# Two steps of TensorE swapped in each slot of a selective scan: the add of h*C before the turn of dt*x*B

## The chip, the cores and the metric

The kernel runs on one core of a Trainium2 chip. The metric is the device time of one execution in microseconds, median of the runs. A core has five engines with an instruction stream each: TensorE (PE in the rows, its weight loads PEld), VectorE (DVE), ScalarE (ACT), GpSimd (POOL) and SyncE (SP, which issues DMAs). They run side by side and meet only at semaphores that the kernel places by hand.

## The reference

A "macaron" layer on x of 4 batches x 512 tokens x 256 channels in float32: a mixture-of-experts FFN, a selective scan (Mamba), the same FFN again. The change is in the scan, of which this is the core:

```python
x_proj = x @ W_x.T
dt_x, Bm, Cm = jnp.split(x_proj, [R, R + N], axis=-1)      # R = 64, N = 16
dt = jax.nn.softplus(dt_x @ W_dt.T + b_dt)
A = -jnp.exp(A_log)
dA = jnp.exp(jnp.einsum('bld,dn->bldn', dt, A))
dBx = jnp.einsum('bld,bln,bld->bldn', dt, Bm, x)
def step(h, inp):
    dA_t, dBx_t, C_t = inp
    h = dA_t * h + dBx_t
    y_t = jnp.einsum('bdn,bn->bd', h, C_t)
    return (h, y_t)
...
y = ys.swapaxes(0, 1) + x * D
```

Around it: `x = x + 0.5 * ffn(layernorm(x))`, then `x = x + scan(layernorm(x))`, then `x = x + 0.5 * ffn(layernorm(x))`.

## The kernel before

The kernel has three stages: the first FFN (to some 183 us of the span), the scan (to some 399 us) and the second FFN. In the scan one batch is worked on after the other (b = 0 to 3), and in each batch one state after the other (n = 0 to 15). State s = 16b + n is one slot; there are 64. For each state, channels lie on the partitions in two halves (k) and 512 tokens lie along them, 1024 elements a partition.

The work of one state s goes over four engines:

- ScalarE (`ahead`, lines 499 to 503), three states on: `decay` makes da = exp(dt*A) (line 482), `outer` makes the product dt*x*B with tokens on the partitions, `dbx_t` (line 496). VectorE makes some of its four token tiles instead (line 998; the table `BY_DVE` says how many).
- TensorE `turn_dbx(s)` (line 730) transposes these four tiles, 8 transposes of 128x128, into one of two PSUM pairs, `DBX[s % 2]`. The pair is read by VectorE's scan of state s-2, so the turn waits for that scan (`sc_h`), and for the products.
- VectorE scans, h = da*h + dbx, over 128x1024 elements in one instruction (line 1012), into a ring of four buffers. It waits for the turn of its state (`sc_dbx`), for da, and for GpSimd to have read the ring buffer of state s-4 (`sc_g`).
- GpSimd multiplies h by C into one of two buffers `gs` (line 381). It waits for the scan, for C's row (a DMA), and for the add of state s-2 (`sc_tp`).
- TensorE `add(s)` (line 745) transposes this product back, again 8 transposes, and sums it over the states in the PSUM pair `YA`. It waits for GpSimd (`sc_g`), and in the first state of a batch for VectorE to have read the sum of the batch before (`sc_x`).

Only states 62 and 63 have their product from VectorE (line 1035). Each engine works through its stream in the written order. In TensorE's slot s (function `scan`, lines 758 to 779) stand: in some slots `project_bt` (n = 4, the B of the next batch turned, lines 691 to 698) or `route` (batch 3, n = 5 and 10, lines 572 to 581); then `turn_dbx(s + 2)`; then `add(s - 1)`; then in some slots more: `project_z` (n = 0, 1), `skip` (n = 3, x*D, 16 matmuls, line 755), `turn_dt` (n = 8, 10), the transposes of LayerNorm (n = 12, 13), `project` (n = 15).

VectorE's slot s: `outer(s + 2)` (its share), scan s, then in some slots more: `add_y` of the batch before (n = 1, line 1042, waits for the last add of that batch), its statistics (n = 2), `project_bt` (n = 4, the copy of the turned B, line 958), `project_w` and `project_dt` (n = 5 to 8, lines 967 to 977), `project_dtx` (n = 10, 12, line 983). GpSimd's slot has the product alone, except in batches 1 to 3 after n = 3: there it also makes the LayerNorm of the batch before (lines 339, 340 and four of line 346).

Of the kernel before, what the change touches and what calls it, by code (L numbers as in the profile page):

```python
# [27 lines left out]
def macaron_kernel(nc, x, w_xT, w_dtT, b_dt, a_log, d_skip, router_w, gate_w, up_w, down_w,  # L28
# [32 lines left out]
    with ExitStack() as ctx:  # L61
# [142 lines left out]
        def states_by(engine, s):  # L204

            return sum(engine in (("dve",) if v else ()) + (("act",) if v < LT else ()) for v in sum(BY_DVE, ())[0:s])

        def last_two(s):

            return s >= STATES - 2  # L210
# [340 lines left out]
        def _(pe):  # L551
            def ln_transposes(c, q):
                pe.wait_ge(ln_xn, GT * c + 2 * q + 2)
                if c == 2:
                    pe.wait_ge(ln_xnT, (GT // 2) * c + q)
                    pe.wait_ge(pj_dtx, 2 * min(q // 2 + 3, BATCH))
                elif c == 1 and q == 7:
                    pe.wait_ge(ln_xnT, GT // 2 + 7)
                elif q >= 2:
                    pe.wait_ge(ln_xnT, (GT // 2) * c + q - 1)  # L560
                dst = turn_bank(c, q)
                for i in range(2):
                    for k in range(KC):
                        last = nc.tensor.transpose(dst[:, (i * KC + k) * P:(i * KC + k + 1) * P],  # L564
                                                   xn[:, 2 * q + i, k * P:(k + 1) * P], ident[:])
                last.then_inc(ln_tp, 1)
# [5 lines left out]
            def route(r, b):  # L572
                c = 2 * r
                if r == 1:
                    pe.wait_ge(sc_dve, states_by("dve", min(N * (BATCH - 1) + (ROUTES + (N, N))[b] + 3, STATES)))
                pe.wait_ge(ln_xnT, (GT // 2) * c + 2 * b + 2)
                for i in range(LT * b, LT * (b + 1)):
                    for k in range(KC):
                        last = nc.tensor.matmul(LG[r][:, i, :], xnT[:, k, i * P:(i + 1) * P], w_rt[:, k, :],  # L579
                                                start=(k == 0), stop=(k == KC - 1))  # L580
                last.then_inc(rt_logits, 1)
# [99 lines left out]
            def project(b):  # L681
                lo = b * L
                pe.wait_ge(ln_xnT, GT // 2 + 2 * b + 2)
                if b > 0:
                    pe.wait_ge(ln_xnT, GT + 2 * max(b - 2, 0))
                    pe.wait_ge(pj_dtx, 2 * b)
                for k in range(KC):
                    mm = nc.tensor.matmul(pj_bank(b, 0)[0:R + 2 * N, :], w_x[:, k, :], xnT[:, k, lo:lo + L], start=(k == 0), stop=(k == KC - 1))  # L688
                mm.then_inc(pj_all, 1)

            def project_bt(b):

                pe.wait_ge(pj_copy, b + 1)
                if b > 0:
                    pe.wait_ge(sc_dve, states_by("dve", N * (b - 1) + 4 + 3))
                for i in range(LT):
                    mm = nc.tensor.transpose(B_T[:, b, i, :], proj[R:R + N, i * P:(i + 1) * P], ident[R:R + N, R:R + N])
                mm.then_inc(pj_bt, 1)

            def project_z(b, k):  # L700
                pe.wait_ge(pj_copy, b + 1)
                if b > 0 and k > 0:
                    pe.wait_ge(pj_max, KC * b + k)
                nc.tensor.matmul(pj_bank(b, k), w_dt[:, k * P:(k + 1) * P], proj[0:R], start=True, stop=True).then_inc(pj_z, 1)

            def turn_dt(b, h):

                pe.wait_ge(pj_dt, KC * (b + 1))
                if b > 0 and h > 0:
                    pe.wait_ge(pj_dtx, 2 * b + h)  # L710
                dst = YS[h] if b == 0 else T
                for i in range(2):
                    for k in range(KC):
                        lo = (b % 2) * L + (2 * h + i) * P
                        mm = nc.tensor.transpose(dst[:, (i * KC + k) * P:(i * KC + k + 1) * P], dt_sb[:, k, lo:lo + P], ident[:])
                mm.then_inc(pj_tp, 1)

            def turn_dbx(s):

                if s >= 2:  # L720
                    pe.wait_ge(sc_h, s - 1)
                elif s == 0:
                    pe.wait_ge(ln_xnT, GT // 2 + 6)
                else:
                    pe.wait_ge(pj_dtx, 2)
                pe.wait_ge(sc_act, states_by("act", s + 1))
                pe.wait_ge(sc_dve, states_by("dve", s + 1))
                for k in range(KC):
                    for i in range(LT):
                        mm = nc.tensor.transpose(DBX[s % 2][:, k, i * P:(i + 1) * P], dbx_t[:, s % TURNS, i, k * P:(k + 1) * P], ident[:])  # L730
                mm.then_inc(sc_dbx, 1)

            def add(s):

                products = gs
                if last_two(s):
                    products = last
                    pe.wait_ge(sc_last, s - (STATES - 3))
                else:
                    pe.wait_ge(sc_g, s + 1)  # L740
                if s % N == 0:
                    pe.wait_ge(sc_x, KC * (s // N))
                for k in range(KC):
                    for i in range(LT):
                        mm = nc.tensor.matmul(YA[k][:, i * P:(i + 1) * P], products[:, s % 2, k, i * P:(i + 1) * P], ident[:],  # L745
                                              start=(s % N == 0 and i == 0), stop=(s % N == N - 1), is_transpose=True, skip_group_check=True)
                mm.then_inc(sc_tp, 1)

            def skip(b):
                lo = b * L  # L750
                if b == 0:
                    pe.wait_ge(consts, 1 + KC)
                for k in range(KC):
                    for i in range(LT):
                        nc.tensor.matmul(YA[k][:, i * P:(i + 1) * P], xnT[:, k, lo + i * P:lo + (i + 1) * P], d_diag[:, k, :],
                                         start=False, stop=False, skip_group_check=True)

            def scan(b):
                more = b + 1 < BATCH
                for n in range(N):  # L760
                    s = N * b + n
                    if more and n == 4:
                        project_bt(b + 1)
                    if not more and n in ROUTES:
                        route(1, ROUTES.index(n))
                    if s + 2 < STATES:
                        turn_dbx(s + 2)
                    if s > 0:
                        add(s - 1)
                    if more and n in (0, 1):  # L770
                        project_z(b + 1, n)
                    if n == 3:
                        skip(b)
                    if more and n in (8, 10):
                        turn_dt(b + 1, (n - 8) // 2)
                    if b > 0 and n in (12, 13):
                        ln_transposes(2, 2 * (b - 1) + n - 12)
                    if n == N - 1 and b + 2 < BATCH:
                        project(b + 2)
# [28 lines left out]
            for b in range(BATCH):  # L808
                scan(b)
# [312 lines left out]
```

## Time and profile before

| what | value |
|---|---|
| runs of the kernel before | 549.12 us median of 3 (547.7 to 549.31) |
| the profiled execution | 548.21 us |
| its span, first to last instruction | 546.4 us |
| mean granted clock of TensorE | 0.926 |
| busy: TensorE, weight loads, VectorE, ScalarE, GpSimd | 80%, 55%, 64%, 47%, 47% |

The rows below come from this one profiled execution. A start is in us from the start of the span. The clock is the share of TensorE's full 2.4 GHz that was granted in a stretch; 0.50 is 1.2 GHz.

### The profile page before, as it was taken

The page shows a single profiled execution, that of the slowest core. Times are in us where ns is not written, and L with a number is a line of the kernel's source. Part 1 is how long each engine was busy: PE and PEld are TensorE (multiplying, and loading weights), DVE is VectorE, ACT ScalarE, POOL GpSimd, SP SyncE. Part 2 cuts the span into 40 slices and gives each one's busy share as a digit, 9 for nine tenths or more (in the row PEclk, how much of TensorE's full clock was granted, in tenths as well). Part 3 has the DMA queues.
Part 4 walks back from the last instruction along what each step waited for, and adds up shares of the span by engine and source line. Part 5 has one row for each costly group of instructions (what it writes and reads, how often), then busy time and mean ns, then how long its engine had stood idle before and what let it go on. Part 6 is the DMA issues. An engine that isn't in the chain of part 4 may idle for free.

```text
span 546.4 us, 7393 instructions
## 1 busy us (share of the span) xinstructions
PE 434.9 (80%) x2204; PEld 301.7 (55%) x2205; DVE 348.1 (64%) x592; ACT 257.6 (47%) x499; POOL 254.6 (47%) x198
## 2 busy tenths in 40 slices
PE   1989989999807477878768867777888998999960
PEld 1745655555404346765667667677763664555530
DVE  5385433343347968999799899997949433333424
ACT  1211122332205769999989999976411112223210
POOL 4117203223321136786979698879802700332230
PEclk9979999999966679899999989997998999999995
DMA  8997312226851012133233223412300331222119
GB/s 266 178 326 247 85 39 78 86 77 197 132 173 60 0 57 75 69 104 90 52 86 96 84 62 98 106 60 78 78 0 30 107 68 41 85 77 86 58 48 307
DMA packets 54188, 55.27 MB, mean 101 GB/s; under 512 B 16465, under 2 KB 43409, under 8 KB 54161
## 3 DMA queue, kind: packets, MB, share of 16 engines
q1 hardware_dynamic: 50416, 44.68, 30.2%
q0 software_dynamic: 3744, 10.24, 5.3%
q8 instruction: 15, 0.25, 0.2%
q14 instruction: 13, 0.10, 0.1%
HBM read 36.39 MB, written 18.52 MB: 100 GB/s over the span
## 4 chain that ended last, share of the span: by engine, by line
PE 53%; DVE 25%; issue 10%; DMA 4%; POOL 3%; ACT 3%; SPq 0%; DVEq 0%; POOLq 0%; ACTq 0%
PE bank L630 16%; DVE hs L1012 12%; PE bank L609 9%; PE bank L655 6%; PE bank L599 5%; PE bank L745 3%; PE bank L730 2%; PE bank L579 2%; DMA xn_no<-token_out 2%; PE bank L564 2%; DVE stats L832 2%; PE bank L688 2%; PE bank L641 2%; PE bank L646 2%; DVE dbx_t L998 2%
## 5 line engine op out<-in xcount | busy, mean ns | idle before, releaser
L381 POOL TENSOR_TENSOR gs<-hs,c_sb 128x1024 f32<-128x1024 f32 x62 | 146.2, 2372 | 43.6 <-DVE hs L1012 32.2
L1012 DVE TENSOR_TENSOR_SCAN hs<-da,bank 128x1024 f32<-128x1024 f32 x64 | 144.8, 2276 | 10.5 <-PE bank L730 10.5
L368 POOL DMA_INDIRECT token_out<-y_sb,row_token x46 | 44.0, 957 | 141.3 <-DVE y_sb L933 141.3
L730 PE MATMUL bank<-ident,dbx_t 128*128 128x128 f32 x512 | 74.0, 291 | 34.1 <-DVE hs L1012 29.3
L630 PE MATMUL bank<-w_gu,tt 128*128 x184 | 90.8, 616 | 3.9 <-ACT tt L433 3.0
L482 ACT ACTIVATE da<-dt_sb,a_neg 128x511 f32<-128x511 f32 x128 | 84.9, 712 | 9.0 <-DVE hs L1012 8.9
L730 PEld LDWEIGHTS bank<-ident,dbx_t 128*128 128x128 f32 x512 | 60.4, 149 | 50.4 <-DVE hs L1012 39.2
L496 ACT ACTIVATE dbx_t<-dtx_t,h_sb 128x256 f32<-128x256 f32 x194 | 83.7, 495 | 3.0 <-PE bank L730 3.0
L921 DVE SCALAR_TENSOR_TENSOR q_sb<-th,bank 128x256 f32<-128x256 f32 x46 | 19.4, 421 | 88.9 <-ACT th L428 88.9
L745 PE MATMUL bank<-ident,gs 128*128 128x128 f32 x496 | 68.7, 285 | 8.7 <-POOL gs L381 8.5
L428 ACT ACTIVATE th<-bank 128x256 f32<-128x256 f32 x46 | 17.6, 383 | 108.4 <-PE bank L630 108.4
L745 PEld LDWEIGHTS bank<-ident,gs 128*128 128x128 f32 x496 | 59.4, 148 | 10.8 <-POOL gs L381 10.4
L609 PE MATMUL bank<-xnT,w_gu 128*128 128x512 f32 x128 | 62.4, 642 | 0.4 <-DVE gs L852 0.4
L630 PEld LDWEIGHTS bank<-w_gu,tt 128*128 128x128 f32 x184 | 31.3, 189 | 40.2 <-issue 40.1
L357 POOL DMA_INDIRECT sorted_rows<-xn_no,slot x32 | 31.2, 975 | 46.5 <-DVE xn_no L895 37.7
L655 PE MATMUL bank<-w_dn,tt 128*128 x184 | 47.8, 382 | 2.5 <-DVE y_sb L933 1.4
L609 PEld LDWEIGHTS bank<-xnT,w_gu 128*128 128x128 f32 x128 | 26.1, 208 | 31.4 <-issue 29.4
L410 ACT ACTIVATE xnT<-bank 128x512 f32<-128x512 f32 x24 | 13.9, 592 | 59.2 <-PE bank L564 59.2
L564 PE MATMUL bank<-ident,xn_no 128*128 128x128 f32 x96 | 18.1, 338 | 29.8 <-DVE xn_no L842 29.0
L421 ACT ACTIVATE hs<-bank 128x512 f32<-128x512 f32 x16 | 9.5, 595 | 61.5 <-PE bank L609 61.5
L655 PEld LDWEIGHTS bank<-w_dn,tt 128*128 128x128 f32 x184 | 31.4, 190 | 6.3 <-issue 4.0
L433 ACT ACTIVATE tt<-bank 128x512 f32<-128x512 f32 (+1 forms) x50 | 28.1, 562 | 9.8 <-PE bank L646 6.2
(103 smaller groups left out, 484.2 us busy)
## 6 DMA issues: line engine op xcount, KB each, us to landing
c_sb<-c_dram SPq DMA_DIRECT2D x64, 256.0 KB, 3.3
sorted_rows<-zero_row SPq DMA_DIRECT2D x2, 2944.0 KB, 17.1
xg<-sorted_rows SPq DMA_DIRECT2D x46, 128.0 KB, 2.0
xn_no<-token_out SPq DMA_DIRECT2D x8, 512.0 KB, 5.6
x_sb<-in_x SPq DMA_DIRECT2D x4, 512.0 KB, 6.5
w_gu<-in_gate_w SPq DMA_DIRECT2D x2, 1024.0 KB, 14.8
w_gu<-in_up_w SPq DMA_DIRECT2D x2, 1024.0 KB, 11.9
w_dn<-in_down_w SPq DMA_DIRECT2D x2, 1024.0 KB, 13.4
```

The lines of the kernel that those rows point to most:

```text
L357: nc.gpsimd.indirect_dma_start(out=sorted_rows[r], out_offset=bass.IndirectOffsetOnAxis(ap=slot[:, i:i + 1], axis=0), in_=xn_no[:, i, :], ...
L368: nc.gpsimd.indirect_dma_start(out=token_out, out_offset=bass.IndirectOffsetOnAxis(ap=row_token[:, j:j + 1], axis=0), in_=y_sb[:, j % 4, : ...
L381: nc.gpsimd.tensor_tensor(gs[:, s % 2], hs[:, s % RING], c_sb[:, s % RING].unsqueeze(1).to_broadcast([P, KC, L]), ALU.mult).then_inc(sc_g, 1)
L482: nc.scalar.activation(da[:, s % RING, k, 1:L], dt_sb[:, k, seq(s // N)][:, 1:L], ACT.Exp, scale=a_neg[:, k, s % N:s % N + 1]).then_inc(sc ...
L496: step = nc.scalar.activation(dbx_t[:, s % TURNS, i, :], dtx_t[:, b % 2, i, :], ACT.Copy, scale=b_t[:, b, i, n:n + 1])
L564: last = nc.tensor.transpose(dst[:, (i * KC + k) * P:(i * KC + k + 1) * P], xn[:, 2 * q + i, k * P:(k + 1) * P], ident[:])
L609: last = nc.tensor.matmul(dst, w_gu[:, k, SHARED, w + fo * P:w + (fo + 1) * P], xnT[:, k, b * L:(b + 1) * L], start=(k == 0), stop=(k == K ...
L630: last = nc.tensor.matmul(H[j0 % 2][:, :], tt[:, j0 % 2, 2 + k], w_gu[:, k, bass.ds(e, 1), :].squeeze(1), start=(k == 0), stop=(k == KC - 1))
L655: last = nc.tensor.matmul(Y[:, 0:D], tt[:, j0 % 2, k], w_dn[:, k, bass.ds(e, 1), :].squeeze(1), start=(k == 0), stop=(k == KC - 1))
L730: mm = nc.tensor.transpose(DBX[s % 2][:, k, i * P:(i + 1) * P], dbx_t[:, s % TURNS, i, k * P:(k + 1) * P], ident[:])
L745: mm = nc.tensor.matmul(YA[k][:, i * P:(i + 1) * P], products[:, s % 2, k, i * P:(i + 1) * P], ident[:], start=(s % N == 0 and i == 0), st ...
L1012: nc.vector.tensor_tensor_scan(hs[:, s % RING].rearrange(flat), da[:, s % RING].rearrange(flat), DBX[s % 2][:, :, :].rearrange(flat), 0.0, ...
```

## The change

In each slot s of TensorE's `scan`, `add(s - 1)` now stands before `turn_dbx(s + 2)`. Both keep their own waits and instructions, and all other engines keep their streams.

```diff
@@ -763,10 +763,10 @@
                         project_bt(b + 1)
                     if not more and n in ROUTES:
                         route(1, ROUTES.index(n))
+                    if s > 0:
+                        add(s - 1)
                     if s + 2 < STATES:
                         turn_dbx(s + 2)
-                    if s > 0:
-                        add(s - 1)
                     if more and n in (0, 1):
                         project_z(b + 1, n)
                     if n == 3:
```

## Rows read from the trace of the kernel before

**Rows 1.** The page, part 1: busy us, share of the span, instructions.

```profile
PE 434.9 (80%) x2204; PEld 301.7 (55%) x2205; DVE 348.1 (64%) x592; ACT 257.6 (47%) x499; POOL 254.6 (47%) x198
```

**Rows 2.** Stretches, batches 1 to 3: start:end, length, each engine's busy time, clock, DMA.

```profile
250.00:302.00 52.00, 40.13 (x301) 34.01 (x300) 48.76 (x49) 47.82 (x93) 43.51 (x22) 0.97 0.34 82
302.00:353.00 51.00, 38.86 (x298) 33.96 (x299) 49.41 (x49) 48.99 (x96) 43.95 (x23) 0.97 0.32 89
353.00:399.00 46.00, 36.86 (x297) 34.41 (x295) 39.70 (x38) 29.24 (x59) 36.28 (x19) 0.93 0.25 69
```

**Rows 3.** Waits of VectorE, 183 to 399: who, for whom, us, times, longest.

```profile
DVE hs L1012 <- PE bank L730: 10.5, 5, 4.6
DVE h_sb L958 <- PE bank L697: 6.7, 3, 2.8
```

**Rows 4.** Timeline, boundary of batches 0 and 1: start, us, instruction, count, idle before.

```profile
249.60 1.28 DVE L1042 TENSOR_TENSOR x_sb<-x_sb,bank 128x512 f32<-128x512 f32 x2 [0.24 <-PE bank L745]
```

**Rows 5.** Timeline, batch 1, states 19 to 23.

```profile
255.61 2.28 DVE L1012 TENSOR_TENSOR_SCAN hs<-da,bank 128x1024 f32<-128x1024 f32 x1
...
257.95 1.97 PE L730 MATMUL bank<-ident,dbx_t 128*128 128x128 f32 x8 [2.48 <-DVE hs L1012]
257.97 2.37 POOL L381 TENSOR_TENSOR gs<-hs,c_sb 128x1024 f32<-128x1024 f32 x1 [2.10 <-DVE hs L1012]
...
261.16 1.95 PE L755 MATMUL bank<-q_sb,xnT 128*128 128x128 f32 x16
...
263.04 0.42 PE L697 MATMUL bank<-ident,th 16*128 16x16 f32 x4
...
263.50 0.23 DVE L958 COPY h_sb<-bank 128x64 f32<-128x64 f32 x1 [2.83 <-PE bank L697]
...
266.63 7.00 POOL L381 TENSOR_TENSOR gs<-hs,c_sb 128x1024 f32<-128x1024 f32 x3
...
267.74 2.28 DVE L1012 TENSOR_TENSOR_SCAN hs<-da,bank 128x1024 f32<-128x1024 f32 x1
269.04 1.09 PE L745 MATMUL bank<-ident,gs 128*128 128x128 f32 x8 [1.38 <-POOL gs L381]
...
271.25 2.27 DVE L1012 TENSOR_TENSOR_SCAN hs<-da,bank 128x1024 f32<-128x1024 f32 x1
```

**Rows 6.** Timeline, batch 2, states 35 to 39.

```profile
310.33 1.09 PE L730 MATMUL bank<-ident,dbx_t 128*128 128x128 f32 x8 [2.48 <-DVE hs L1012]
...
311.26 1.04 PE L745 MATMUL bank<-ident,gs 128*128 128x128 f32 x8
...
321.43 1.17 PE L745 MATMUL bank<-ident,gs 128*128 128x128 f32 x8 [2.80 <-POOL gs L381]
...
322.22 2.28 DVE L1012 TENSOR_TENSOR_SCAN hs<-da,bank 128x1024 f32<-128x1024 f32 x1
```

**Rows 7.** Timeline, batch 3, states 55 to 57.

```profile
367.73 1.07 PE L730 MATMUL bank<-ident,dbx_t 128*128 128x128 f32 x8
...
368.83 2.29 DVE L1012 TENSOR_TENSOR_SCAN hs<-da,bank 128x1024 f32<-128x1024 f32 x1 [0.44 <-PE bank L730]
...
371.78 1.97 PE L745 MATMUL bank<-ident,gs 128*128 128x128 f32 x8 [2.98 <-POOL gs L381]
373.54 1.91 PE L730 MATMUL bank<-ident,dbx_t 128*128 128x128 f32 x8
...
375.49 2.29 DVE L1012 TENSOR_TENSOR_SCAN hs<-da,bank 128x1024 f32<-128x1024 f32 x1 [4.06 <-PE bank L730]
...
378.02 2.29 DVE L1012 TENSOR_TENSOR_SCAN hs<-da,bank 128x1024 f32<-128x1024 f32 x1
```

**Rows 8.** Timeline, the end of the scan: state 60, then 61 to 63 merged.

```profile
385.80 2.29 DVE L1012 TENSOR_TENSOR_SCAN hs<-da,bank 128x1024 f32<-128x1024 f32 x1 [0.44 <-PE bank L730]
...
388.31 6.63 DVE L1012 TENSOR_TENSOR_SCAN hs<-da,bank 128x1024 f32<-128x1024 f32 x3
```

**Rows 9.** Stretch after the gap in batch 2: length, TensorE busy, granted clock, DMA.

```profile
322.40:325.70 3.30, 3.30 (x18) 0.50 0.44 113
```

## The prediction

> **What bounds the kernel now.** I first read the busy shares of the page: no engine is busy all the time, VectorE 64% of the span [rows 1]. The change touches only the selective scan, so the next view is the table of stretches, one for each batch of the scan. In the middle two batches VectorE is busy 49 of 51 to 52 us, GpSimd 44 and TensorE 40; in the last batch VectorE has only 39.7 of 46.0 [rows 2]. So the scan is paced by VectorE's own list, and what costs time is what makes VectorE wait. The table of waits lists these for the whole scan: 10.5 us for TensorE's turned products of line 730 (five times) and 6.7 us for the turned B of line 697 (three times) [rows 3]. All other waits on TensorE are free. The question is thus where `turn_dbx(s + 2)` comes later or earlier, and whether a VectorE scan is ready for it then.
>
> **The loop in rows.** I number states 0 to 63 (s = 16b + n). From the start of scan s to the start of what it releases (turn, product h*C) pass 2.34 us: 255.61 to 257.95 [rows 5]. From the start of a product to the start of its add pass 2.41 us: 266.63 to 269.04 [rows 5]. A block of 8 transposes at full clock moves the next block back by 0.93 us: 310.33 to 311.26 [rows 6]. From the start of a turn to the scan that waited for it pass 1.10 us: 367.73 to 368.83 [rows 7]. At half clock the two last terms together are read directly: add at 371.78, turn at 373.54, scan at 375.49, that is 3.71 us [rows 7], against 0.93 + 1.10 = 2.03 us at full clock.
>
> **What the change does in an undisturbed slot.** Before, turn s+2 waits for scan s alone. After, it also stands behind add s-1, and so behind product s-1. From the start of scan s-1: 2.34 + 2.41 + 2.03 = 6.78 us until scan s+2 can start. VectorE itself needs three scans with their outer products for this, at 2.53 us (375.49 to 378.02 [rows 7]) 7.59 us, more where it also has projection work. The tightest place is the last three scans: 388.31 + 6.63 - 2.28 = 392.66 us for the start of scan 63, less 385.80 for scan 60, 6.86 us [rows 8]. So the new wait is covered everywhere, in the end by under 0.1 us. In return adds move into TensorE's idle time before the scan's end. Cost of the undisturbed slots: 0. If this cover goes (TensorE at half clock, or a product 0.3 us late), the price is up to 1.7 us a slot.
>
> **Gain at batch boundaries.** In slots 16 and 32 the last add of a batch releases VectorE's addition of y (line 1042), which waits 0.24 us for it [rows 4]. Now this add comes before its turn (0.93 us earlier): -0.24 us, twice, since the row at 301.98 repeats it.
>
> **Gain at the turned B.** In slot 16b+3 add 16b+2 stands between turn 16b+5 and the skip matmuls, behind which come the turned B and VectorE's copy (line 958). The product for this add is done 2.10 us before scan 16b+3 ends (GpSimd's idle time before 257.97 [rows 5]), so the add moves into idle time. In batch 1 the copy at 263.50 comes at 257.95 - 0.24 + 0.93 + 1.88 + 0.46 = 260.98, where 1.88 is skip to turned B (261.16 to 263.04) and 0.46 turned B to copy (to 263.50) [rows 5]; half clock at 257.95 gave 1.97 us in place of 1.09 and is part of the 2.5 us. In batch 2 it gains 0.93 us. In batch 0 TensorE is behind anyway, both orders hold the same work ahead of the B, and the gain is 0.
>
> **Loss at GpSimd's LayerNorm.** In batches 1 to 3, after product 16b+3, GpSimd normalises the batch before (lines 340, 346): in batch 1 from the end of product 19 at 257.97 + 2.37 = 260.34 to 266.63, so product 16b+4 is 6.3 us late and its add starts at 269.04 [rows 5], 321.43 [rows 6] and 371.78 [rows 7]. Before, that add is behind turn 16b+7, and only turn 16b+8 is held up. After, turn 16b+7 is held up too, one scan earlier. VectorE is one scan less ahead of GpSimd, and this is where that counts.
>
> The clock decides the price. TensorE would now wait from turn 16b+6 until the add, about 6 us in batches 1 and 2 (batch 1: the B turned from 260.52, then add 19 and turn 22 until 262.8, then nothing until 268.8), and 4.9 in batch 3, where turn 55 no longer fills the gap. In the trace the gap of 2.80 us before 321.43 and that of 2.98 us before 371.78 were both followed by half the granted clock (0.50, the 1.2 GHz level; blocks of 1.9 us) for 3.3 us and more [rows 6, 7, 9]; in batch 1 the wait of 1.38 us was not [rows 5]. Longer gaps than those that did it, so I take 3.71 us in all three; the other end is 2.03. The Trainium skill ("TensorE: Matmul & The Clock Gate", section "Why this matters for your kernels") says that idle gaps between bursts throw TensorE back to half rate; the trace agrees at the two gaps named. By that rule the sum is the one below, without it the second rival's.
>
> Batch 1: scan 23 starts at 269.04 - 0.24 + 3.71 = 272.51, before 271.25: **+1.26** (boundary gain within; the gain at the turned B is gone, as scan 23 waits for TensorE in any case). After it VectorE has 3.51 us a slot (267.74 to 271.25) and nothing is late.
> Batch 2: the add starts 1.26 - 0.24 = 1.02 later, at 322.45, scan 39 at 326.16, before 322.22: 3.94, of which **+2.68** is new.
> Batch 3: it has no boundary gain, as TensorE has no projection there. The add starts at 371.78, now followed by turn 55 and not 56. So scan 55 starts at 375.49 in place of 368.83, and scan 56 follows by VectorE's pace at 378.02 in place of 375.49: **+2.53**. The old stall of 4.06 us is not repeated for scan 56, its turn is done by then. The rest of batch 3 keeps VectorE's pace: 0.
>
> Sum: 1.26 + 2.68 + 2.53 = +6.47 us. The profiled execution took 548.21 us with its span of 546.44 us, 0.9 below the median of 549.12. 548.21 + 6.47 = 554.7 in its terms, 555.6 in those of the median, 1.2% slower. The second FFN is not touched; its half-clock stretches may fall otherwise, which I put at 1 us either way (each of 3.3 us costs at most half of that).
>
> **Rivals.**
> 1. *The tight cover breaks* (slower still). The slack of under 0.1 us at the tail and of 0.8 elsewhere is gone wherever TensorE is at half clock: 6.78 + 1.68 = 8.46 against 7.59 us. For: the restarts leave it at half clock for a slot or two. Against: in batches 1 and 2 these slots hold 3.5 us of VectorE work each. Two such slots and a late tail are 2 to 3 us: 558.
> 2. *The clock stays up* (about the same). Every restart at 2.03 us: batch 1 270.83 - 271.25 = -0.42; batch 2 adds -0.24 + 1.24 = 1.00; batch 3 2.53 - 1.68 = 0.85; sum +1.43: 550.6. Against: both shorter gaps. One full-clock restart of three would give 553.9.
> 3. *Faster: the earlier B counts.* If scan 16b+7 did not wait for GpSimd, the copies would give 2.52 us in batch 1 and 0.24 + 0.93 = 1.17 us in batch 2, with batch 3 unchanged: -3.69, 545.4. This decides at the start of product 16b+4: it would have to start by 271.25 - 2.52 - 2.03 - 2.41 = 264.3 in batch 1, and starts at 266.63 [rows 5]. Only a LayerNorm 2.3 us shorter or later in its place would do.
> 4. *The change does nothing*, as TensorE passes a turn ahead of a waiting add: 549.1. Against: turn 56 needed only scan 54, done before scan 55 began at 368.83, and yet came after the add, at 373.54 [rows 7]. The Trainium skill (same page, "Part 2: What happens when you issue a matmul") has only weight loads pulled ahead and matmuls in program order. The rows say the same of a turn behind an add that waits.
>
> **Chances.** Forecast 0.74, rival 1 0.10, one or two restarts at full clock 0.05, rival 2 0.04, rival 3 0.04, rival 4 0.03. The forecast's own range is 553.5 to 557.5: the clock may come back within a turn (-0.8 each), the FFN, and 0.8 us between runs. With rival 1 and the mixed case 552.0 to 558.0; rivals 2 to 4 stay out. 0.3% is 1.6 us, about what a measurement of this kernel can tell from no change: slower than 550.8 are the forecast, rival 1 and the mixed case (0.89), within 0.3% rivals 2 and 4 (0.07), faster rival 3 (0.04).
>
> **What would show it.** In the trace after, scans 23, 39 and 55 each wait for line 730, in batch 3 for some 7 us in place of 0.44, and scan 56 for nothing; the three adds after a gap of 5 to 6 us are at half clock; the copy of line 958 waits under 1 us in batches 1 and 2; VectorE waits nowhere else; the scan ends some 6.5 us later. Wrong would be: full clock after the gaps, VectorE waits of 0.5 us and more in slots with n of 8 and more, or GpSimd starting product 16b+4 at another distance from product 16b+3 than 8.7 us.

## The result, and the profile after

The changed kernel took 558.17 us (median of 4 runs, 557.74 to 558.44) against 549.21 in the same comparison: a ratio of 1.0163, 95% interval 1.0126 to 1.020. That is slower, as forecast, but 2.6 us above the predicted 555.6, 0.17 above the range (552.0 to 558.0) and 0.67 above the forecast's own part of it (553.5 to 557.5). Two later comparisons of the same kernel gave 1.0117 (1.0057 to 1.0176) and 1.0091 (1.0056 to 1.0126); over all 16 runs the median is 556.25 us, from 553.2 to 561.1. The profiled execution after took 557.74 us, its span is 556.0.

The waits of VectorE between 183 and 410 us, in the kernel after (who, for whom, us in total, times, longest; the last line is the addition of y behind the last scan, where before had 1.7 us in three waits, longest 1.2):

```profile
DVE hs L1012 <- PE bank L730: 21.5, 6, 7.1
DVE h_sb L958 <- PE bank L697: 2.7, 3, 1.6
DVE x_sb L1042 <- PE bank L745: 2.4, 1, 2.4
```

Against [rows 3] the wait for the turned products doubled, and that for the turned B fell by 4.0 us. One of the six waits for turned products, 5.60 us at scan 2, lies in batch 0; before it was 4.61. GpSimd, TensorE and VectorE in batch 1, the timeline that answers [rows 5] (start, length, instruction, count, idle before):

```profile
260.11 2.38 POOL L381 TENSOR_TENSOR gs<-hs,c_sb 128x1024 f32<-128x1024 f32 x1 [2.10 <-DVE hs L1012]
...
263.35 0.23 DVE L958 COPY h_sb<-bank 128x64 f32<-128x64 f32 x1 [0.54 <-PE bank L697]
...
267.60 2.28 DVE L1012 TENSOR_TENSOR_SCAN hs<-da,bank 128x1024 f32<-128x1024 f32 x1
268.80 6.99 POOL L381 TENSOR_TENSOR gs<-hs,c_sb 128x1024 f32<-128x1024 f32 x3
...
271.21 1.97 PE L745 MATMUL bank<-ident,gs 128*128 128x128 f32 x8 [6.00 <-POOL gs L381]
272.97 1.91 PE L730 MATMUL bank<-ident,dbx_t 128*128 128x128 f32 x8
...
274.92 2.29 DVE L1012 TENSOR_TENSOR_SCAN hs<-da,bank 128x1024 f32<-128x1024 f32 x1 [3.73 <-PE bank L730]
```

Product 20 starts 8.69 us after product 19 (8.66 before). Add 20 waits for it behind a gap of 6.00 us, and turn 23 behind the add: scan 23 starts 3.71 us after the add began. In batch 2 the same rows stand at 324.78, 326.54 and 328.49. In batch 3 the turn now held up is that of scan 55; the answer to [rows 7]:

```profile
378.06 1.97 PE L745 MATMUL bank<-ident,gs 128*128 128x128 f32 x8 [4.79 <-POOL gs L381]
379.83 1.62 PE L730 MATMUL bank<-ident,dbx_t 128*128 128x128 f32 x8
381.28 1.04 PE L745 MATMUL bank<-ident,gs 128*128 128x128 f32 x8
381.48 2.29 DVE L1012 TENSOR_TENSOR_SCAN hs<-da,bank 128x1024 f32<-128x1024 f32 x1 [7.07 <-PE bank L730]
...
384.00 2.28 DVE L1012 TENSOR_TENSOR_SCAN hs<-da,bank 128x1024 f32<-128x1024 f32 x1
```

And what [rows 4] showed is gone, the addition of y follows scan 17 without a wait:

```profile
251.77 1.26 DVE L1042 TENSOR_TENSOR x_sb<-x_sb,bank 128x512 f32<-128x512 f32 x2
```

**The balance by stretches.** I cut each trace at starts of VectorE's scans, which are in its timeline. All numbers are us between two scans' starts; "outside" is the span less the stretch from scan 0 to scan 63, good to about 0.1 us.

| kernel | 0 to 17 | 17 to 18 | 18 to 23 | 33 to 34 | 34 to 39 | 49 to 56 | 56 to 63 | 0 to 63 | outside |
|---|---|---|---|---|---|---|---|---|---|
| before | 59.33 | 4.05 | 20.12 | 4.05 | 18.70 | 25.05 | 17.17 | 204.91 | 341.5 |
| after | 59.77 | 3.71 | 21.64 | 3.70 | 21.64 | 27.28 | 17.14 | 211.34 | 344.7 |
| after, again | 59.43 | 3.70 | 21.62 | 3.70 | 21.62 | 27.57 | 17.15 | 211.24 | 340.5 |
| after, third | 59.33 | 3.70 | 21.64 | 3.71 | 21.59 | 27.59 | 17.14 | 211.15 | 343.4 |
| swapped at n = 5 only | 59.27 | 4.06 | 21.61 | 4.05 | 21.23 | 27.58 | 16.57 | 210.81 | 343.0 |
| batch 0 and n > 8 | 59.43 | 3.99 | 20.19 | 3.99 | 18.71 | 25.08 | 18.95 | 206.76 | 341.0 |
| the same, not in batch 3 | 60.03 | 3.99 | 18.71 | 3.99 | 18.71 | 25.08 | 17.19 | 204.13 | 343.6 |
| n = 0 and n = 3 only | 60.21 | 3.70 | 17.85 | 3.70 | 17.84 | 25.06 | 16.57 | 201.94 | 344.4 |
| after, TensorE kept busy | 59.25 | 3.70 | 19.94 | 3.70 | 19.94 | 25.87 | 17.15 | 206.01 | 344.7 |
| after, LayerNorm spread | 59.76 | 3.71 | 17.84 | 3.70 | 17.85 | 23.58 | 19.43 | 202.30 | 346.4 |
| before, LayerNorm spread | 59.36 | 4.06 | 20.13 | 4.05 | 18.72 | 20.92 | 21.25 | 204.91 | 341.4 |
| n = 0, 3, LayerNorm spread | 60.09 | 3.70 | 17.85 | 3.70 | 17.84 | 20.13 | 21.18 | 200.92 | 343.4 |
| the same, again | 59.82 | 3.70 | 17.83 | 3.70 | 17.84 | 20.13 | 21.17 | 200.62 | 343.8 |

The stretches 23 to 33 and 39 to 49 take 28.2 to 28.5 us in every kernel. So of the 9.6 us by which the span grew, 6.4 lie in the scan (-0.34, +1.52, -0.35, +2.94, +2.23, and +0.44 in batch 0), and 3.2 outside it, where no line was changed. Batch 0 also differs where its order is the same. Its first two scans take 13.03 us at a granted clock of 0.68 before, and 14.02 us at 0.51 after; in the third trace of the changed kernel they take 13.02 us at 0.68 again, and in the kernel of experiment 2, with the old order in batch 0, 14.15 us at 0.62. So the +0.44 us goes with where the half clock fell, and not with the order.

### The profile page after: what moved, and what is told of

Same layout as the page of the kernel before. It is cut to its first block, busy times and chain, and to the rows that moved or that the text cites. A ratio compares the mean times of both kernels' runs of the same rounds, so it can differ in the third digit from the quotient of the medians.

```text
span 556.0 us, 7393 instructions
## 1 busy us (share of the span) xinstructions
PE 441.4 (79%) x2204; PEld 307.7 (55%) x2205; DVE 348.0 (63%) x592; ACT 257.9 (46%) x499; POOL 255.2 (46%) x198
## 4 chain that ended last, share of the span: by engine, by line
PE 53%; DVE 25%; issue 9%; POOL 7%; DMA 4%; ACT 2%; SPq 0%; DVEq 0%; POOLq 0%; ACTq 0%
PE bank L630 16%; DVE hs L1012 14%; PE bank L609 10%; PE bank L655 6%; PE bank L599 5%; POOL gs L381 3%; PE bank L745 3%; PE bank L579 3%; PE bank L730 2%; POOL xn_no L346 2%; DVE dbx_t L998 2%; DMA xn_no<-token_out 2%; PE bank L564 2%; DVE stats L832 2%; PE bank L641 2%
## 5 line engine op out<-in xcount | busy, mean ns | idle before, releaser
L745 PE MATMUL bank<-ident,gs 128*128 128x128 f32 x496 | 71.4, 290 | 39.2 <-POOL gs L381 36.7
L745 PEld LDWEIGHTS bank<-ident,gs 128*128 128x128 f32 x496 | 58.1, 148 | 53.5 <-POOL gs L381 45.1
L730 PE MATMUL bank<-ident,dbx_t 128*128 128x128 f32 x512 | 72.6, 289 | 6.7 <-DVE hs L1012 3.5
L730 PEld LDWEIGHTS bank<-ident,dbx_t 128*128 128x128 f32 x512 | 62.7, 150 | 11.2 <-DVE hs L1012 6.4
L564 PE MATMUL bank<-ident,xn_no 128*128 128x128 f32 x96 | 18.3, 339 | 29.3 <-DVE xn_no L842 28.5
```

## The experiments

**1. The three slots alone.** The edit, here and in the next two experiments with other conditions:

```diff
+                    add_first = b > 0 and n == 5
+                    if add_first and s > 0:
+                        add(s - 1)
                     if s + 2 < STATES:
                         turn_dbx(s + 2)
-                    if s > 0:
+                    if not add_first and s > 0:
                         add(s - 1)
```

> The two steps are swapped in three slots only, those of batches 1 to 3 with n = 5, where the add waits for the product behind GpSimd's LayerNorm. Theory A (the whole loss is one turn held up at the LayerNorm, three times): batch 1 269.04 + 3.71 - 271.25 = +1.5, batch 2 321.43 + 3.71 - 322.22 = +2.9, batch 3 +2.2 to +2.5; sum +6.6 to +6.9 from scan 0 to scan 63, so a little more than the full change, since the gains at the turned B and at the batch boundaries are missing. Rival B (the new order costs a little in each slot): 3 of 61 slots, under 0.5 us.

Measured: 558.23 us, ratio 1.0142 (1.0092 to 1.0192), 555.60 us in the profiled execution, and +5.9 us from scan 0 to scan 63: +1.49, +2.53 and +2.53 in the three batches, -0.60 at the end. Three of 61 slots carry the loss. It is under my 6.6 to 6.9 because TensorE's clock came back sooner in batch 2, already within the turn that followed the add (timeline, TensorE, this kernel; the second row holds two blocks of turns and half of it is at full clock):

```profile
324.92 1.97 PE L745 MATMUL bank<-ident,gs 128*128 128x128 f32 x8 [3.43 <-POOL gs L381]
326.68 2.39 PE L730 MATMUL bank<-ident,dbx_t 128*128 128x128 f32 x16
```

and because the end, from scan 56 to scan 63, is 0.60 us shorter; 0.44 of it is the wait for turn 60, which is gone.

**2. The gains alone.** `add_first = b > 0 and n in (0, 3)`.

> The two steps are swapped only in batches 1 to 3 at n = 0 (last add of a batch, for which VectorE waits) and n = 3 (the turned B of the next batch comes behind them). Theory A: only the gains are left. Batch 1 0.34 + 2.3, batch 2 0.34 + 0.87, batch 3 nothing: -3.85 us, 545.4 us in all. Rival B (the gain is taken back at the LayerNorm, as GpSimd then is late by more): -0.7 us at most, the two boundary gains.

Measured: 546.04 us, ratio 0.9939 (0.9909 to 0.9968), and 17 to 18 and 18 to 23 together 2.62 us shorter, 33 to 34 and 34 to 39 1.21: -3.83, as theory A had it. In the sum 0 to 63 some 0.9 of it is missing again in batch 0 (60.21 in place of 59.33), where the order is the old one: the start of the scan at half clock, see above. Two smaller terms nearly cancel: 23 to 33 and 39 to 49 are 0.29 us longer each (28.50 for 28.21, add 20 and add 36 being at half clock), and 56 to 63 is 0.60 shorter. Of the 2.27 us in batch 1, 1.41 is not the order's for certain: it is the half clock at 257.95 in [rows 5], and the kernel "the same, not in batch 3" has the old order there, did not fall to half clock, and took 18.71 us. The order alone gives 0.87 us, as in batch 2. The copy of the turned B waits as little as in the full change, and scan 23 is not held up, since turn 23 stands ahead of add 20 (timeline of this kernel):

```profile
263.36 0.23 DVE L961 COPY h_sb<-bank 128x64 f32<-128x64 f32 x1 [0.55 <-PE bank L697]
...
266.43 1.09 PE L730 MATMUL bank<-ident,dbx_t 128*128 128x128 f32 x8 [1.21 <-DVE hs L1015]
...
271.12 2.28 DVE L1015 TENSOR_TENSOR_SCAN hs<-da,bank 128x1024 f32<-128x1024 f32 x1
271.18 1.97 PE L745 MATMUL bank<-ident,gs 128*128 128x128 f32 x8 [3.66 <-POOL gs L381]
```

**3. The slots that I had called undisturbed.** `add_first = b == 0 or n > 8`.

> The two steps are swapped in batch 0 and in batches 1 to 3 from n = 9 on, not in the slots around the LayerNorm, the turned B and the batch boundary. Theory A (undisturbed slots are covered): from scan 0 to scan 63 within 0.5 us of before. Rival B (the tight cover breaks where slack is under 0.1 to 0.8 us, in the last scans of batch 3 above all): +1 to +3 us, with waits of VectorE for line 730 in slots of n = 9 and more.

Measured: 549.61 us, ratio 1.0019 (0.9991 to 1.0046), but +1.85 us from scan 0 to scan 63, of it +1.78 in 56 to 63, the end of batch 3. Here theory A failed and rival B was right in its size, yet not for slack under 0.1 us. The timeline shows what it was:

```profile
380.13 2.28 DVE L1015 TENSOR_TENSOR_SCAN hs<-da,bank 128x1024 f32<-128x1024 f32 x1
381.62 1.09 PE L745 MATMUL bank<-ident,gs 128*128 128x128 f32 x8 [1.23 <-POOL gs L381]
382.55 1.04 PE L730 MATMUL bank<-ident,dbx_t 128*128 128x128 f32 x8
...
383.63 2.29 DVE L1015 TENSOR_TENSOR_SCAN hs<-da,bank 128x1024 f32<-128x1024 f32 x1 [1.22 <-PE bank L730]
```

GpSimd works off what the LayerNorm left behind until the end of batch 3, so product 56 is late, add 56 waits 1.23 us for it, and turn 59 stands behind it. In the full change this stretch takes 17.14 us, as before, since VectorE has lost its lead already at scan 55.

> As the kernel quiet_slots, which swapped the two steps in batch 0 and from n = 9 on and took 206.76 us from scan 0 to scan 63 in place of 204.91, but with batch 3 left in the old order. Theory A (the swapped slots cost only where GpSimd is behind, and there alone in the end of batch 3): 204.9 within 0.2 us. Rival B (undisturbed slots cost a little each, and the tail only shows it): over 205.5.

Measured: 549.51 us, ratio 1.000 (0.9976 to 1.0024). 56 to 63 is 17.19 us again, and batches 1 and 2 take from n = 9 on what they took. Theory A holds: it costs nothing in these slots outside the end of batch 3. (The whole stretch is 204.13, since 18 to 23 did not have the half clock of [rows 5] at 257.95, -1.41, and batch 0 had some, +0.70.)

**4. The clock's share.** The changed kernel, and ahead of the add at n = 5:

```diff
+            def keep_warm(count):
+                for i in range(count):
+                    nc.tensor.matmul(YA[0][:, 0:P], zero_row[:, 0:P], ident[:], start=False, stop=False,
+                                     is_transpose=True, skip_group_check=True)
...
+                        if b > 0 and n == 5:
+                            keep_warm((0, 44, 44, 34)[b])
                         add(s - 1)
```

> The changed kernel, and in the three slots with n = 5 of batches 1 to 3 TensorE transposes a tile of zeros into the sum of y 44, 44 and 34 times before the add that waits for GpSimd; the zeros change nothing, and at 0.11 us each they end before the product does. So the gaps of 6.0, 6.0 and 4.8 us are work. Theory A (hold-up plus the half clock after the gap): add, turn and scan then take 2.03 us in place of 3.71 (3.42 in batch 3); the stretch from scan 0 to scan 63 falls from 211.3 to 206.4 us, and +1.5 us against before (204.9) is left, which is the hold-up itself less the gains. Rival B (the clock doesn't matter, GpSimd alone sets the pace behind the LayerNorm): 211.3 again.

Measured: 551.38 us, ratio 1.0024 (0.9998 to 1.0050); 206.01 us from scan 0 to scan 63, 5.3 under the changed kernel. Its timeline in batch 1:

```profile
264.70 4.97 PE L751 MATMUL bank<-ident,zero_row 128*128 128x128 f32 x44
...
270.87 1.09 PE L745 MATMUL bank<-ident,gs 128*128 128x128 f32 x8 [1.20 <-POOL gs L381]
271.80 1.04 PE L730 MATMUL bank<-ident,dbx_t 128*128 128x128 f32 x8
272.87 2.29 DVE L1022 TENSOR_TENSOR_SCAN hs<-da,bank 128x1024 f32<-128x1024 f32 x1 [2.02 <-PE bank L730]
```

From add to scan 2.00 us in place of 3.71. Of the 5.3 us, 4.8 lie in the three stretches with a gap (1.70, 1.70 and 1.41) and 0.5 in batch 0, which this edit does not touch; against the two later traces of the changed kernel the three stretches make 5.1. So of the 6.0 us that the change costs from batch 1 on, 4.8 are the half clock. The 1.2 left are the hold-up less the gains: as the gains are 3.8 (experiment 2), the hold-up itself is an estimated 5.0 at full clock, as large as the clock's share. 122 matmuls of zeros, work for nothing, make the changed kernel faster (a ratio of 1.0024 to the kernel before, where it had 1.0091 to 1.0163). Whether they would also speed up the kernel before, which has half-clock stretches of its own [rows 9], was not tried.

**5. The cause of the late product.** GpSimd's LayerNorm one tile behind each of the products n = 3 to 6, instead of all four behind n = 3:

```diff
                     if b > 0 and n == 3:
                         rstd_of(2, b - 1)
-                        normalise(2, b - 1)
+                    if b > 0 and n in (3, 4, 5, 6):
+                        normalise_tile(2, b - 1, n - 3)
```

With the changed order:

> The changed order, with GpSimd's LayerNorm spread: reciprocal root and first tile behind product n = 3, one tile behind each of the products n = 4, 5, 6, so no product is 6.3 us late. Theory A (the loss is the product behind the LayerNorm block): batch 1 and 2 show only the gains (2.6 and 1.2 us), batch 3 about 0; from scan 0 to scan 63 201 us, 3.9 under before and 10 under the changed kernel. Rival B (the new order itself costs): above 205 us still.

Measured: 548.41 us, ratio 0.9976 (0.9944 to 1.0008); 202.30 us, 9.0 under the changed kernel. In batches 1 and 2 the loss is gone to the last 0.01 us (17.84 as in experiment 2), although every slot has the new order: so the slots n = 1, 2, 4, 6, 7 and 8, which no experiment swapped alone, cost nothing there. Batch 3 (49 to 63) is 43.01 against 42.22 before: +0.8, where I had about 0.

With the old order:

> The order of before, with the same spread LayerNorm. Theory A: batches 1 and 2 as before, as nothing waited there; in batch 3 the wait of 4.06 us for turn 56 goes, but GpSimd stays the bound of the tail, so scan 63 comes some 2 us earlier: 202.9 us from scan 0 to scan 63. Rival B (GpSimd's total decides batch 3): no change, 204.9.

Measured: 549.12 us, ratio 0.9992 (0.9956 to 1.0029), and 204.91 us from scan 0 to scan 63, as before to the digit. Rival B. The wait of 4.06 us before scan 56 went (49 to 56 is 4.13 shorter), and came back to 4.08 between 56 and 63. So that wait was not the bound of batch 3. In its place the trace shows GpSimd, whose rows follow one another with no gap over 0.1 us from 360.11 to 385.06 us, while VectorE's scans 58, 59 and 60 wait 0.80, 1.24 and 1.30 us (timeline, this kernel):

```profile
375.75 9.31 POOL L387 TENSOR_TENSOR gs<-hs,c_sb 128x1024 f32<-128x1024 f32 x4
376.64 2.29 DVE L1022 TENSOR_TENSOR_SCAN hs<-da,bank 128x1024 f32<-128x1024 f32 x1 [0.80 <-PE bank L737]
```

With the order unchanged, GpSimd's products and LayerNorm together set the length of batch 3, wherever the LayerNorm stands. With other orders of TensorE the stretch is 41.3 to 44.7 us, so it is not GpSimd's work alone.

**6. Both, and more runs.**

> The add first only at n = 0 and n = 3 of batches 1 to 3, and the LayerNorm spread. Theory A: the gains of both add: 2.6 + 1.2 + 2.0 = 5.8 us under before, 199.1 us from scan 0 to scan 63, 543.3 in all. Rival B (GpSimd with 3.57 us a slot in n = 3 to 6 becomes the bound of batches 1 and 2, now that VectorE comes earlier): 3 us or less under before.

Measured: 543.76 us, ratio 0.9891 (0.9842 to 0.9939), 200.92 us in the scan, 4.0 under before and not 5.8; 1.1 of the 1.8 us missing is batch 3 (41.31 against 42.22, -0.9 where I had -2.0), for the reason shown in experiment 5 with the old order; the rest is batch 0 (60.09). Neither theory had the size. GpSimd did not become the bound of batches 1 and 2 (17.84 us, as without the spread).

> The version with the add first only at n = 0 and n = 3 of batches 1 to 3 and the LayerNorm spread, once more, for its time: 200.9 us from scan 0 to scan 63 as in its first trace, 4.0 us under before; in all 543 to 546 us, a ratio of 0.989 to 0.995 to before.

Measured: 546.07 us, ratio 0.9916 (0.9888 to 0.9944), 200.62 us in the scan. This version beats both kernels: it has the add first where VectorE waits for an add or for what comes behind it, and nowhere else.

> The changed kernel once more, unchanged. In its trace the first scan of the selective scan starts 2.05 us later than before (189.80 against 187.75), though nothing ahead of it was changed; from there to the start of scan 63 it takes 211.34 us against 204.91, and another 1.2 us more by the addition of y after the last scan. Theory A (chance): the 2.05 us come from where TensorE's half-clock stretches fell in the first FFN, and vary from execution to execution; the stretch from scan 0 to scan 63 is again 6.0 to 6.5 us longer than before, the whole 6.5 to 9 us longer. Rival B (systematic): scan 0 starts at 189.8 again in this execution and the whole is again 9 us longer.

Measured: 553.47 us (553.24 to 561.09); 211.24 us in the scan, 340.5 outside. Scan 0 starts at 187.28 us, and not at 189.80. The stretch of the scan is theory A's, the whole is not: 4.5 us over before by the medians and 5.2 by the profiled executions, where theory A had 6.5 to 9.

> The changed kernel a third time. Two traces of it show 211.34 and 211.24 us from scan 0 to scan 63 (before 204.91), but 344.66 and 340.46 us outside it (before 341.49), and 557.74 and 553.40 us in all. Theory A: the stretch of the scan is a property of the order, 211.3 again within 0.4; what lies outside it is chance and again anywhere in 340 to 347, so whole times of 552 to 561 us with most of them below 558. Rival B: what lies outside depends on the kernel too, and most executions give 558 as the first four did.

Measured: 555.11 us (553.22 to 557.43); 211.15 us in the scan, 343.4 outside. The scan's stretch repeats within 0.2 us, and what lies outside it does not: chance, as theory A had it in both. The first TensorE work of the FFN, 16 to 34 us, in the traces of before, after and after again (stretch, length, TensorE busy, granted clock, DMA):

```profile
16.00:34.00 18.00, 16.32 (x94) 0.85 0.98 208
```

```profile
16.00:34.00 18.00, 16.32 (x90) 0.68 0.96 196
```

```profile
16.00:34.00 18.00, 16.32 (x93) 0.85 1.01 220
```

The kernel with 344.7 us outside had the clock at 0.68 there, and its 32 small matmuls of the router took 6.83 us against 3.84 before. Over the whole stretch ahead of scan 0 the granted clock and the length go together: 187.75 us at 0.91 before, 189.80 at 0.88 after, and 192.95 at 0.88 in the longest trace (changed order, LayerNorm spread), with the same 555 matmuls in each. And after the last scan its two final adds were at half clock:

```profile
404.59 3.42 PE L745 MATMUL bank<-ident,dbx_t 128*128 128x128 f32 x16 [1.94 <-DVE dbx_t L1035]
```

In the second trace of the same kernel the two took 2.23 us, after the same wait of 1.94:

```profile
401.96 2.23 PE L745 MATMUL bank<-ident,dbx_t 128*128 128x128 f32 x16 [1.94 <-DVE dbx_t L1035]
```

## Why the prediction was right or wrong

**The hold-up at the LayerNorm: right.** The forecast had scans 23, 39 and 55 wait, and scan 56 no more. They did, with 3.73, 3.73 and 7.07 us. From the end of the batch boundary on, the terms were 1.50 for batch 1, 2.92 for batch 2 and 2.53 for batch 3; measured 1.52, 2.94 and 2.23, and 2.52 to 2.54 in the two later traces. In the first the clock came back within the turn (3.42 us from add to scan, not 3.71), which I had named. Experiment 1 shows that these slots carry the loss, experiment 5 that the late product causes it, and experiment 4 that of the 6.0 us from batch 1 on the half clock makes 4.8. One reading was loose: the add after the gap of 2.80 us in [rows 6] still took 1.17 us, and the clock was 0.50 only from 322.40 on [rows 9]. The longer gaps of the change gave half clock from the add's start.

**The gains: right.** 0.34 us a boundary where I had 0.24: the addition of y follows without a wait, so it also overlaps the scan before it by some 0.1 us. The earlier B gave 2.3 and 0.87 us where I had 2.28 (2.52 with the boundary) and 0.93, seen in experiment 2, where nothing takes it back. In the change itself it was lost in the wait of scans 23 and 39, as forecast. For the whole stretch of the scan I had +6.47 us; measured were 6.43, 6.33 and 6.24. That the first is so near is luck: it has the 0.44 us of batch 0, which was not in my sum, and without it is 5.99. The 2.28 of batch 1 also rests on the half clock at 257.95, without which the order gives 0.87.

**The untouched parts: this step failed.** I put what lies outside the scan at 1 us either way, by half-clock stretches of 3.3 us that cost at most half of that each, and considered the second FFN alone. Over thirteen traces it took 340.5 to 346.4 us with no line of it changed (341.5 in the profile of before), and batch 0, where the new order costs nothing, 59.25 to 60.21. In the profiled execution after, this made +3.2 us outside, 2.05 of it ahead of scan 0, in the first FFN, which I had left out. The execution lies 3.0 us above the sum in its own terms (557.74 for 554.7), and the 3.2 us account for it; the +0.44 of batch 0 was offset by smaller terms in the scan. The term is of a size with half the change. Reckoned after the fact from these traces it is -1.1 to +5.8 us with batch 0, so 553.6 to 560.5 about 554.7; the 16 runs lie between 553.2 and 561.1.

**"Undisturbed slots cost 0, by under 0.1 us of cover": right in the sum, wrong in its reason.** I took VectorE's pace of 6.86 us for three scans against 6.78 as the test. That holds only where GpSimd is not behind. In the tail of batch 3 it is, and there the swap costs 1.8 us if VectorE still has its lead (experiment 3). In the full change it cost nothing there (17.14 us). My reading is that the lead was lost at scan 55 already, and that the one cost is not paid twice; no run separates the two.

**The rivals.** Rival 2 (full clock) was the right price for a case that did not come by itself: +1.43 us, and with TensorE kept busy it was +1.10 from scan 0 to scan 63. Rival 3 (faster) failed at the point that it named, the start of product 20; with the swap at n = 0 and n = 3 alone the kernel is the faster one, and the swap everywhere but at n = 5 was not run. Rival 1's place was real, its cause another. Rival 4 did not occur: turn 23 ran behind add 20, at 272.97, though in experiment 2, with scan 21 at the same time (264.09), it ran at 266.43.

## What to carry to other kernels

In an in-order stream that feeds the pacing engine, ask of each step what it can be made to wait for, not only how long it takes: a step of 0.9 us put ahead of the critical one costs nothing until its own producer is late once, and then it hands on the whole delay. Swap only in the slots where someone waits for the step (here n = 0 and n = 3), and look at the producer's rarest, longest piece of work first. And where a clock can halve after a gap, price a new gap by the work behind it, and measure how much untouched parts vary from execution to execution before giving a range.

## What was not expected of the hardware

- Matmuls of zeros in a gap paid, in the changed kernel: with 4.97 us of them in gaps of 6.0 us, the granted clock stayed at 1.00 and add and turn took 2.00 us to the scan, not 3.71.
- The same 16 matmuls behind the same wait of 1.94 us ran at half clock in one execution (3.42 us) and at full in the next (2.23 us). Gaps of 3.4 us and more in the scan's slots n = 5 were always followed by half clock.
- With the same instructions, the parts outside the scan took 340.5 to 346.4 us in thirteen traces. What decides in which execution the router's matmuls at 25 us fall into a half-clock stretch, and why the first four runs all lay near 558 us, stays open; it was not tried.
